# Step sums spread over three PSUM banks, one-hot matrices four deep, and the loop's other work re-spaced

## What is computed

```python
xn = _layernorm(x)                                   # x: 6250 x 256
# graph part: 200000 edges, 32 relations, 8 bases, dst sorted
weight = einsum('rb,bio->rio', w_comp, bases)
msg = einsum('ni,rio->nro', xn, weight)[src, rel_type] * norm
gnn = relu(segment_sum(msg, dst, num_segments=6250))
# mixer: 8 heads of 32
Q = elu(xn @ Wq) + 1; K = elu(xn @ Wk) + 1; v = xn @ Wv
KV = einsum('nshd,nshv->nhdv', K, v)
Z = 1 / (einsum('nlhd,nhd->nlh', Q, K.sum(1)) + 1e-6)
m = _layernorm(einsum('nlhd,nhdv,nlh->nlhv', Q, KV, Z) @ Wm, g1, b1)
h = relu(concatenate([xn, m]) @ W1) @ W2
x = x + gnn + xn + _layernorm(h, g2, b2)
# experts, on xe = _layernorm(x); all eight for every row
w = softmax(xe @ Wr + br)
y = three layers of 256x256 per expert (bias, norm, relu after the first two)
return x + einsum('bfed,fe->bfd', y, w)
```

## Time and profile before

| | |
|---|---|
| median of 3 runs | 4206.27 us (4196.62 to 4210.25) |
| the profiled execution | 4209.15 us, its span 4207.4 us |
| PE busy | 3357.9 us, 80% of the span |
| DVE busy | 2255.9 us, 54% |
| POOL busy | 1949.4 us, 46% |
| ACT busy | 800.3 us, 19% |
| DMA | 205 GB/s over the span |

### The profile page before, as it was taken

One profiled execution on the slowest core, in us unless ns is written; L12 is line 12 of the kernel. 1 busy time (PEld: TensorE's weight loads), 2 busy tenths in 40 slices (PEclk: granted clock), 3 DMA queues, 4 the chain that ended last, 5 costly groups with the idle time before them and its releaser, 6 DMA issues.

```text
span 4207.4 us, 68614 instructions
## 1 busy us (share of the span) xinstructions
PE 3357.9 (80%) x18778; PEld 2955.5 (70%) x18778; DVE 2255.9 (54%) x6008; ACT 800.3 (19%) x1546; POOL 1949.4 (46%) x2001
## 2 busy tenths in 40 slices
PE   0179976686988889898898888888888888888887
PEld 0157765575877868788787787877877778777675
DVE  5634465555555565555555555555555555555422
ACT  0023420001112121121211212112121221211233
POOL 0132246655555555555555555555454555555100
PEclk9999987887999999999899998998989999899899
DMA  6467776666766667676676766767667676676532
GB/s 195 128 194 237 241 206 189 198 194 207 235 206 219 211 219 239 201 230 208 210 232 208 229 210 209 228 217 226 204 210 231 214 219 216 208 237 207 163 103 80
DMA packets 647245, 864.29 MB, mean 205 GB/s; under 512 B 63829, under 2 KB 524195, under 8 KB 646686
## 3 DMA queue, kind: packets, MB, share of 16 engines
q1 hardware_dynamic: 510962, 549.74, 40.0%
q0 software_dynamic: 95776, 262.27, 21.8%
q10 hardware_dynamic: 40140, 47.81, 3.4%
HBM read 551.97 MB, written 316.84 MB: 206 GB/s over the span
## 4 chain that ended last, share of the span: by engine, by line
PE 53%; issue 11%; DVE 9%; another core or an unknown queue 5%; ACT 3%; DVEq 1%; SPq 0%; DMA 0%; ACTq 0%
PE PS L1674 53%; DVE steps L1306 4%; ACT feed L926 1%; DVE steps L1270 1%; DVE feed L1602 1%; ACT h_high L925 0%; ACT mixbuf L902 0%; DVE h_low L1005 0%; PE PS L1743 0%; ACT mixbuf L896 0%; DVE lst L1415 0%; DVE mixbuf L1437 0%; DVE lnr L1005 0%; DVE mixbuf L1005 0%
## 5 line engine op out<-in xcount | busy, mean ns | idle before, releaser
L746 POOL DMA_INDIRECT steps<-normed_nodes,steps x1968 | 1931.2, 981 | 1781.9 <-PE PS L1674 877.3
L1306 DVE SCALAR_TENSOR_TENSOR steps<-steps,PS 128x256 f32<-128x256 f32 x1968 | 944.7, 480 | 1599.5 <-PE PS L1674 1107.1
L1674 PE MATMUL PS<-steps 128*128 128x128 f32 x7872 | 1267.4, 299 | 316.6 <-issue 133.3
L1674 PEld LDWEIGHTS PS<-steps 128*128 128x128 f32 x7872 | 1169.1, 211 | 422.6 <-issue 257.7
L926 ACT ACTIVATE feed<-PS,bnc 128x512 f32<-128x512 f32 x416 | 319.9, 774 | 825.5 <-PE PS L1674 547.4
L1674 PE MATMUL PS<-bases_s,feed 128*128 128x256 f32 x1664 | 440.7, 408 | 0.0
L1674 PEld LDWEIGHTS PS<-bases_s,feed 128*128 128x128 f32 x1664 | 416.4, 334 | 6.2
L1270 DVE TENSOR_TENSOR steps<-steps 128x512 f32<-128x512 f32 x494 | 337.3, 683 | 0.1
L1674 PE MATMUL PS<-w_one,feed 128*128 128x256 f32 (+1 forms) x1028 | 309.5, 427 | 5.8 <-ACT feed L926 5.8
L925 ACT ACTIVATE h_high<-PS,bnc 128x512 fp32r<-128x512 f32 x208 | 161.6, 777 | 794.5 <-PE PS L1674 724.4
L1674 PE MATMUL PS<-h_high,split_in 128*128 128x512 f32 x832 | 276.0, 458 | 16.8 <-ACT feed L926 16.7
(11 more groups left out here) (208 smaller groups left out, 2881.3 us busy)
## 6 DMA issues: line engine op xcount, KB each, us to landing
step_sums<-steps SPq DMA_DIRECT2D x492, 512.0 KB
split_in<-expert_split SPq DMA_DIRECT2D x104, 1024.0 KB
feed<-step_sums SPq DMA_DIRECT2D x416, 128.0 KB
steps<-step_types SPq DMA_DIRECT2D x125, 256.0 KB
steps<-normed_nodes,steps POOLq DMA_INDIRECT x1968
mixbuf<-mix_hidden SPq DMA_DIRECT2D x53, 256.0 KB
w_zero<-in_L_ffn_Wo_dram SPq DMA_DIRECT2D x52, 256.0 KB
w_one<-in_L_ffn_Wo_dram SPq DMA_DIRECT2D x52, 256.0 KB
```

The source lines that it names most:

```text
L746: pool.indirect_dma_start(out=ring[:, k, :], out_offset=None, in_=xnD, in_offset=bass.IndirectOffsetOnAxis(ap=idxc[:, u, k:k + 1], axis=0) ...
L1306: dve.scalar_tensor_tensor(acc[:, k % ACCR, :], acc[:, (k - 1) % ACCR, :], keepc[:, k:k + 1], PS[:, slot(k):slot(k) + C], ALU.mult, ALU.ad ...
L1674: return pe.matmul(o, a, b, start=start, stop=stop)
```

## The change

- `slot` now rotates the pairs over banks 0, 1 and 7, and a pair's matmuls wait for the pair of three before; in M1, which needs bank 7, two banks stay in use (`few`).
- `selm` holds all four parts. The selects stand at p=4, 5 and 7 for parts 0, 1 and 2 of the next iteration, and p=1 for part 3; `coefs` and `dst_hot` move to p=3, `rel_hot` prepares two iterations ahead at p=6, `coef_mm` moves from step 10 to step 1. The buffer comes from the destination field of the table, kept in bfloat16 (`places`), and from one M1 buffer less.
- The experts begin each 17 steps. `third` writes bank 6 only, in two halves of which the second stands eight steps behind the first; `LATE` shifts the halves of the first three experts. Layers and third layer have loads of their own.
- The bases' product stands behind steps 8 to 11 of an iteration instead of 2 to 5, with a wait for `coefs` of the next iteration, since both use bank `B_ONE`. `sum_up` moves from p=4 to p=7. The router's work moves into the block before.
- The mixer's products and DVE parts in the loop stand at new steps (`MIX_36`); in the mix stage they stay (`MIX_32`). SP's load of edge types moves from step 6 to step 14.

```diff
-EXP_AT = SPAN // EXPERTS
+EXP_AT = 17
+LATE = (5, 3, 1, 0, 0, 0, 0, 0)
-M1_BUFS = 4
+M1_BUFS = 3
-ALEAD = 3
+ALEAD = 5
...
+        STEP_BANKS = (0, 1, 7)
-        def slot(k):
-            return (k % 4) * C
+        def slot(u, k, few):
+            pair = u * (UN // 2) + k // 2
+            return (pair % 2 if few else STEP_BANKS[pair % 3]) * 512 + k % 2 * C
...
-                wait_apart(sp, "f_l3", LEAD + done)
+                wait_apart(sp, "f_l2", LEAD + 2 * done)
...
             def ahead(it, p, u):
                 if p == 0:
-                    indices(it + 1, u + 1)
+                    indices(it + 2, u + 2)
                 if p == 1:
-                    select(it, 2, s + BATCH + RING)
-                if p == 2:
-                    rel_hot(it + 1)
+                    select(it, 3)
                 if p == 3:
-                    select(it, 3, s + 2 * BATCH + RING)
-                if p == 5:
                     coefs(it + 1)
                     dst_hot(it + 1)
+                if p == 4:
+                    select(it + 1, 0)
+                if p == 5:
+                    select(it + 1, 1)
                 if p == 6:
-                    select(it + 1, 0, s + 3 * BATCH + RING)
+                    rel_hot(it + 2)
                 if p == 7:
-                    select(it + 1, 1, s + 4 * BATCH + RING)
-                    dve.wait_ge(sem("acc_done"), s + UN + ALEAD)
+                    select(it + 1, 2)
+                    dve.wait_ge(sem("acc_done"), it * UN + UN + ALEAD)
                     keeps(it + 1)
...
+            MIX_32, MIX_36 = (0, 4, 5, 2, 3, 6, 8, 13), (2, 4, 5, 5, 5, 10, 11, 16)
...
+                            if at == (EXP_AT * e + 7) // 2:
+                                hidden_low(fed, e)
+                            if at == (EXP_AT * e + 21 + LATE[e]) // 2:
+                                o_add(fed, e, (0, 1))
+                            if at == min((EXP_AT * e + 29 + LATE[e]) // 2, SPAN // 2 - 1):
+                                o_add(fed, e, (2, 3))
+                    if prep and 1 <= i <= SUP and p == 7:
+                        sum_up(b, i - 1, fed)
...
-                    pe.wait_ge(sem("acc_done"), s - 2 + ALEAD)
+                    pe.wait_ge(sem("acc_done"), s - (2 if few else 4) + ALEAD)
...
+            MIX_32, MIX_36 = (2, 9, 12, 20, 22, 25, 29), (6, 12, 16, 25, 28, 29, 35)
...
-                return bank(B_O + j // 2, (j % 2) * C, (j % 2) * C + C)
+                return bank(B_O, (j % 2) * C, (j % 2) * C + C)
             def third(fed, e, j):
                 if j == 0:
                     pe.wait_ge(sem("f_h2"), LEAD + 2 * EXPERTS * fed + 2 * e + 2)
-                if j % 2 == 0:
-                    pe.wait_ge(sem("o_upd"), LEAD + SUP * (EXPERTS + 1) * fed + SUP * e + j + 2)
+                    pe.wait_ge(sem("o_upd"), LEAD + SUP * (EXPERTS + 1) * fed + SUP * (e + 1))
+                if j == 2:
+                    pe.wait_ge(sem("o_upd"), LEAD + SUP * (EXPERTS + 1) * fed + SUP * (e + 1) + 2)
...
+                            if r in (0, 1):
+                                first(fed, e, r)
+                            if r in (9, 10):
+                                second(fed, e, r - 9)
+                            if r - LATE[e] in (15, 16):
+                                third(fed, e, r - LATE[e] - 15)
+                            if r - LATE[e] in (23, 24):
+                                third(fed, e, r - LATE[e] - 21)
+                    if prep and 8 <= k < 12 and i > 0:
+                        if k == 8 and it0 is not None and i != 5:
+                            pe.wait_ge(sem("coef_ready"), LEAD + it + 2)
+                        if i <= SUP:
+                            combine(b, i - 1, k - 8)
```

More of the change, by code:

```diff
@@ L594, in mix_it, with block_its @@
                         load_hidden(n + 1, nxt)
-            def block_its(it0, b, s, fed):
+            def block_its(it0, b, s, fed, prep):
                 for at in range(SPAN):
                     i, k = divmod(at, UN)
-                    e, r = divmod(at, EXP_AT)
                     j, m = divmod(at, MIX_AT)
[L602 to L621, removed]
@@ new lines, in block_its @@
+                    if it0 is not None:
+                        it = it0 + i
+                        if k % BATCH == BATCH - 1:
+                            keep_steps(it, k)
+                        if k == 14:
+                            next_types(it)
+                        tile = s[0] * SUP + j
+                        nxt = s[0] * SUP + j + 1 if j < SUP - 1 else s[1] * SUP
+                        n = SUP * b + SUP + j
+                        if m == 9:
+                            load_query(n + 1, nxt)
+                        if m == 14:
+                            load_shift(n, tile)
+                        if m == 35:
+                            load_hidden(n + 1, nxt)
@@ new lines, in block_its @@
+                    if fed is None and at == 104:
+                        load_third(0, 0)
+                    if fed is None and at == 108:
+                        load_layers(0, 1)
+                    if fed is not None:
+                        for e in range(EXPERTS):
+                            if at == EXP_AT * e + 12 and (prep or e < EXPERTS - 2):
+                                load_layers(EXPERTS * fed + e + 1, (e + 2) % EXPERTS)
+                            if at == (EXP_AT * (e - 1) + 31 if e else 6) and (prep or e < EXPERTS - 1):
+                                load_third(EXPERTS * fed + e, (e + 1) % EXPERTS)
@@ L959, in block_its @@
                     i, k = divmod(at, UN)
-                    e, r = divmod(at, EXP_AT)
                     j, m = divmod(at, MIX_AT)
                     n = SUP * b + SUP + j
-                    if fed is not None and r == 1:
-                        hidden(fed, e, 0)
-                    if fed is not None and at == 3:
-                        act.wait_ge(sem("r_tp"), fed + 1)
-                        act.copy(wt[:, :], bank(B_O)[0:EXPERTS, :]).then_inc(sem("r_wt"), 1)
-                    if m == 2 and (mixed or prep and j == 0):
+                    if fed is not None:
+                        for e in range(EXPERTS):
+                            if at == EXP_AT * e + 1:
+                                hidden(fed, e, 0)
+                            if at == EXP_AT * e + 10:
+                                hidden(fed, e, 1)
+                        if at == 6:
+                            act.wait_ge(sem("r_tp"), fed + 1)
+                            act.copy(wt[:, :], bank(B_O)[0:EXPERTS, :]).then_inc(sem("r_wt"), 1)
@@ L1288, in _ @@
             indices(0, 0)
-            for q in range(2):
-                select(0, q, RING)
+            indices(1, 1)
+            for q in range(3):
+                select(0, q)
+            rel_hot(1)
             dve.wait_ge(sem("grow_in"), 32)
@@ L1391, in _ @@
                     m1_q(TILES - 2 + p)
-                pair(it, p)
+                pair(it, p, it, True)
                 if p == 0:
@@ new lines, in block_its @@
+                    if prep and 8 <= k < 12 and i > 0:
[3 more added lines that the diff above has]
+                            combine(b, i - 1, k - 8)
+                        if i in (6, 7) and k == 8:
+                            row_turn(b, 2 * (i - 6))
+                        if i == BLK - 1 and k == 8:
+                            logits(b)
+                    if prep and i in (6, 7) and k == 12:
+                        row_turn(b, 2 * (i - 6) + 1)
```

304 lines of the change are left out of this document (150 added, 154 removed).

## The result

The changed kernel takes 4379.0 us (4365.16 to 4380.83, 4 runs) against 4208.26 for the kernel before, a ratio of 1.040 (95% interval 1.037 to 1.043). Three more comparisons, each beside the kernel before on another chip, gave 1.045, 1.045 and 1.042 (mean of the four 1.043). The forecast was 4082, with a range up to 4280.

What follows compares the result with a forecast made beforehand. The loop, 70% of the span, was taken as PE's work plus its gaps. From 4209.15 us, loop -74, mix stage and block 0 -25, tail -25 gave 4085, or 4082 by the median; range 3960 to 4280, likeliest 4020 to 4150.

Steps and rivals of the forecast that it cites:

- The tail: After the loop: each of 16 experts loses its 1.54 us wait for the first hidden layer, -25 us.
- The step waits: Loop: a third bank and four `selm` parts remove PE's waits ahead of steps, -10.7 us per block.
- The new waits: Loop: products now one step behind their DVE cause make PE wait, +10 us per block.
- the sum before its discount: Loop: added waits for messages, `coefs`, `o_add` and `sum_up`, 14.5 us per block before two thirds were taken.
- The clock: Loop: fewer long gaps leave PE less time at half speed, -6 us per block.
- Mix stage and block 0: Before the loop: a third of the 71.8 us of step waits goes, -25 us.
- B: Rival, loop: one-step waits outweigh the removed ones, slower, 4276 us; chance 0.20.
- E: Rival: sums are late because DVE sees a pair's end late, not for want of banks; about 4195 us; chance 0.18.
- D: Rival, loop: more and shorter gaps lower the granted clock from 0.93 to 0.86, 4285 us; chance 0.05.
- C: Rival, loop: nearly all step gaps and 12 us of clock go, new waits cost 5; 3930 to 3980 us; chance 0.12.

Runs made afterwards that it cites:

- e1: The changed kernel with step sums in two banks instead of three, run twice: 4409 and 4393 us, ratios 1.028 and 1.029 to the kernel before.
- e8_all: The changed kernel, three banks kept, with `o_add`/`o_begin`, `hidden_low` and messages earlier and the bases' product later: 4104 us, ratio 0.9753 to the kernel before.
- e4b: Second run of the changed kernel with bases' product, row turns and logits behind steps 10 to 13 instead of 8 to 11: 4369 us, ratio 1.022.
- e6: The changed kernel with the messages and their reciprocal behind a tile's fourth pair instead of the sixth: 4391 us, ratio 1.0445 to the kernel before.
- e10: e8_all with `tail_moments` one pair earlier on DVE and `mix_hidden` moved earlier on ACT: 4116 us, ratio 0.978 to the kernel before.
- e3: The changed kernel with `o_add` of both halves and the first half's `o_begin` one pair earlier on DVE: 4316 us, ratio 1.009 to the kernel before.
- e3b: Second run of e3's edit to the changed kernel, on another chip: 4316 us, ratio 1.010 to the kernel before.

## Where the prediction was right and where it failed

- **The tail**, -25, was -28.3. The 1.54 us wait is gone and an expert takes 4326.51 - 4315.92 = 10.6 us, where the forecast said 10.8:

```profile
4315.92 1.27 PE L1705 MATMUL PS<-x1t_high,split_in 128*128 128x512 f32 x4
...
4324.90 1.96 PE L1705 MATMUL PS<-w_one,feed 128*128 128x256 f32 x8 [0.92 <-issue]
4326.51 1.29 PE L1705 MATMUL PS<-x1t_high,split_in 128*128 128x512 f32 x4
```

- **The step waits**, -10.7 per block, went almost wholly: from 316.6 to 43.8 us over the span. In the loop the gaps ahead of steps fell from 207.8 to 16.3 us, per block from 18.9 to 1.5. The direction was right and the size too small. But e1 shows that most of this is no credit to the third bank: with two banks they come back to 122.1 and 133.5 us only, while PE is held up elsewhere.
- **The new waits**, +10 per block, are the step that failed. The rows in the loop: `o_add` 123.1/11 = 11.2 per block (I had 5), `coefs` 6.2 (3.5), the messages 2.7 with a name and 3.3 more without (5), `h_low` 5.4 (I had nothing). Only `sum_up` went the other way: 1.3 for the shared bank's read, where I had 2.7 + 1. With what the rows of before had there, that is some 27 per block more, where the sum before its discount was 14.5.
  - Two kinds of place were left out. For `o_add` I priced the second halves of the third layer, 8 per block, at 5 us, and they measure 56.6/11 = 5.1. The first halves, which since the change wait for the second `o_add` of the expert before, I gave nothing; they measure 66.5/11 = 6.0, of which expert 1 alone has 3.4. That wait is in the diff. `h_low` is not: the change only moved its two ends, and I listed the waits that the diff adds and not the pairs of places whose distance it changes.
  - The price of a place was also short: one pair and one operation against one step, 0.7 us for `coefs`. The rows say 68.5/41 = 1.7 for `coefs` and 59.1/20 = 3.0 for `h_low`; in the example above `mix_moments` stands between as well.
  - Taking two thirds of the sum, on the ground that waits overlap, was a discount for which no row spoke.
- **The clock**, -6 per block, was +6.5. I let the clock rise because the long gaps ahead of steps would go. They went, and longer ones came at other places: gaps of 2.5 us and more from 51 to 91 in the loop, and the time at half clock from 423 to 601 us. In e8_all they are 44 and 410, at the 0.93 of the kernel before.
- **Mix stage and block 0**, -25, was -10.7. The clock stayed at 0.79, and POOL's 20 us per iteration was not reached: 24.5 and 25.8 us. I let a third of the 71.8 us of step waits go. In fact 61.6 went (L1323 has 10.2 left, `select` none), and other waits took most of it: 17.6 for the messages and 17.7 for L1453, where they were 1.3 and 9.9. It is the loop's exchange on a small scale.
- **The rivals**: B was right in kind, with the price of its name too low: I wrote +4.5 us per block as the point at which the new waits decide, and they exceeded it by far. E is out by its sign, since the rows of the sums did not stay. D's sign did come, a fall of the clock to 0.90 and 71 us of busy time, a third of what D had; but it is not the rotation that makes it (e1). In the sums, C takes 8 us of clock where its text says 12, and B takes 40 us for the other stages and 50 in the next sentence; neither bears on the forecast. The chance of 0.20 for B rested on "DVE is busy 57% of the loop, so it is seldom far behind". A busy share says nothing of how many steps lie between a product and its user.

## What to carry to other kernels

When engines run written-out orders, list every producer and consumer pair that the change moves, also those without a new wait and those that a shared buffer ties across two rounds (here expert 0's sums and expert 1's third layer), and count for each the work in both queues between them. That list, and not the share of busy time, tells where gaps can come. It does not tell their length, nor that each will come: by the table experts 1 and 3 have `h_low` as close to `second` as 5 and 7 have it, and never waited in the changed kernel's trace. And when a wait goes and the time does not fall, look where the same time came back before calling the edit worthless: e4b, e6 and e10 each show such an exchange.

## What was not expected of the hardware

The kernel before took 4208 to 4215 us on most chips and 4272 and 4282 us on two, 1.5% more. No other kernel ran on both kinds of chip (e3 and e3b, 4316 and 4316, are of the two slower ones), so whether only the kernel before is sensitive to the chip no run here settles.

DVE's 209.4 us of waits have no releaser in the profile's rows, but the trace's semaphore records show one. In all 66 of them `mm_done`, which PE raises at the end of a step, is updated within 0.3 us before DVE starts, and this update comes 1.9 to 9.5 us (median 4.6) after the recorded end of the step's last matmul; over all pairs whose update is recorded just before DVE starts, the median is 0.01 us. In the example at 1955.73 above, the two steps' updates are at 1957.14 and 1959.35, and DVE starts at 1959.46. So DVE is not late there: either PE's products run later than the rows show, or their end is told late, and some of PE's gaps behind such a place are shorter than they look. The reason stays open. Re-spacing (e8_all) left 167.1 us of these waits in nearly the same loop.
